# Cross attention and routed FFN on one core: another buffer order at the end of attention, two late loads of the first batch behind its context, and the second column chunk in reverse token order

## The reference

```python
def xattn(query, key):
    a = einsum('bqd,bkd->bqk', query, key)
    return einsum('bqk,bkd->bqd', softmax(a), key)

def ffn(x, base_w, base_b, A, B, router_w):      # base_w 2048x2048, A 64x2048, B 16x2048x64
    base_out = einsum('bsi,oi->bso', x, base_w) + base_b
    res_hidden = einsum('bsi,ri->bsr', x, A)
    probs = softmax(einsum('bsi,ei->bse', x, router_w))
    topw, topi = top_k(probs, 2); topw = topw / (sum(topw) + 1e-6)
    combine = sum(one_hot(topi, 16) * topw[..., None], axis=-2)
    return base_out + 0.5 * einsum('bse,bsr,eor->bso', combine, res_hidden, B)

x = x + xattn(layernorm(x), ctx)
x = x + ffn(layernorm(x), ...)
```

## Time and profile before

| | |
|---|---|
| time, median of 3 runs | 1458.26 us (1456.08 to 1459.49) |
| the profiled execution: its time, its span | 1453.22 us, 1451.5 us |
| PE busy | 1365.1 us, 94% of the span |
| DVE, ACT, POOL busy | 950.6, 634.3, 325.4 us |
| mean granted PE clock | 0.985 |
| mean DMA rate | 242 GB/s |

### The profile page before, as it was taken

How to read it: one execution, slowest core, us unless ns; L and a number is a source line. 1 busy time by engine, 2 the same in 40 slices (tenths; PEclk the granted TensorE clock), 3 DMA queues, 4 the chain that set the end, 5 groups by cost and what they waited for, 6 DMA issues and landing times.

```text
span 1451.5 us, 18409 instructions
## 1 busy us (share of the span) xinstructions
PE 1365.1 (94%) x6777; PEld 1107.6 (76%) x6777; DVE 950.6 (65%) x1199; ACT 634.3 (44%) x797; POOL 325.4 (22%) x247
## 2 busy tenths in 40 slices
PE   5899999999999999999799988899989999999998
PEld 4678787787878787787688766677767788888886
DVE  6486777777687767768355467676767746445553
ACT  3355554545564554545311266677767501100100
POOL 2002002020201102020414724444445011111110
PEclk9899999999999999999999999999999999999999
DMA  9958678687867768679656698999996987887874
GB/s 323 271 179 261 198 255 252 202 249 235 276 213 250 231 223 253 211 251 178 198 166 173 185 280 268 264 313 293 302 308 166 359 250 240 254 256 240 257 246 130
DMA packets 216840, 350.59 MB, mean 242 GB/s; under 512 B 26992, under 2 KB 129392, under 8 KB 207088
## 3 DMA queue, kind: packets, MB, share of 16 engines
q1 hardware_dynamic: 198192, 282.31, 64.5%
q0 software_dynamic: 10528, 52.85, 11.7%
q10 hardware_dynamic: 8064, 14.68, 2.9%
HBM read 266.11 MB, written 99.41 MB: 252 GB/s over the span
## 4 chain that ended last, share of the span: by engine, by line
PE 35%; DMA 13%; DVE 3%; issue 2%; ACT 1%; SPq 1%; POOL 0%; POOLq 0%; ACTq 0%; DVEq 0%
PE scores L829 11%; PE scores L830 10%; PE scores L831 10%; DMA res<-x_scratch 7%; DMA y_scratch<-y_out,yrow_i 3%; DMA w_in<-in_wT_dram 2%; PE work L865 1%; PE work L866 1%; DMA a_in<-xT_scratch 1%; DVE w_l L1382 1%; DVE raw_l L1148 1%; ACT y_out L1054 1%; ACT b_hl L1046 0%; DMA hs_scratch<-hg,pos_i 0%; DVE x L1184 0%
## 5 line engine op out<-in xcount | busy, mean ns | idle before, releaser
L829 PE MATMUL scores<-w_h,a_h 128*128 128x512 f32 x896 | 354.5, 396 | 14.0 <-DVE a_l L1389 8.1
L831 PE MATMUL scores<-w_h,a_l 128*128 128x512 f32 x896 | 352.4, 393 | 0.0
L830 PE MATMUL scores<-w_l,a_h 128*128 128x512 f32 x896 | 352.4, 393 | 0.0
L1030 ACT ACTIVATE a_h<-a_in 128x512 fp32r<-128x512 f32 x168 | 94.3, 621 | 317.5 <-DMA a_in<-xT_scratch 210.5
L1389 DVE TENSOR_TENSOR a_l<-a_in,a_h 128x512 fp32r<-128x512 f32 x168 | 130.7, 826 | 127.2 <-ACT a_h L1030 123.1
L829 PEld LDWEIGHTS scores<-w_h,a_h 128*128 128x128 f32 x896 | 169.7, 189 | 53.6 <-issue 15.2
L831 PEld LDWEIGHTS scores<-w_h,a_l 128*128 128x128 f32 x896 | 169.5, 189 | 38.3
L830 PEld LDWEIGHTS scores<-w_l,a_h 128*128 128x128 f32 x896 | 169.7, 189 | 37.1
L695 PE MATMUL scores<-ctxT_h,nT_h 128*112 128x494 f32 (+1 forms) x512 | 174.9, 342 | 10.6 <-DVE ctxT_l L1138 6.2
L1148 DVE TENSOR_TENSOR raw_l<-raw_in,val_h 128x512 fp32r<-128x512 f32 x192 | 155.0, 826 | 44.8 <-ACT val_h L959 44.6
L1557 POOL TENSOR_TENSOR res<-res,bias_b 128x512 f32<-128x512 f32 x56 | 86.4, 1543 | 407.9 <-DMA res<-x_scratch 388.0
(11 more groups left out here) (149 smaller groups left out, 1977.8 us busy)
## 6 DMA issues: line engine op xcount, KB each, us to landing
ctxT_in<-in_ctxT_dram SPq DMA_DIRECT2D x64, 750.0 KB, 7.6
a_in<-xT_scratch SPq DMA_DIRECT2D x42, 1024.0 KB, 8.7
raw_in<-in_ctx_dram SPq DMA_DIRECT2D x32, 1280.0 KB
w_in<-in_wT_dram SPq DMA_DIRECT2D x32, 512.0 KB, 9.6
x<-in_x_dram SPq DMA_DIRECT2D x8, 1792.0 KB, 9.3
xT_scratch<-xT_st SPq DMA_DIRECT2D x8, 1792.0 KB, 11.8
res<-x_scratch SPq DMA_DIRECT2D x56, 256.0 KB, 7.7
y_add<-y_scratch SPq DMA_DIRECT2D x56, 256.0 KB, 5.3
```

The lines of the kernel that those rows point to most:

```text
L829: pe.matmul(o, ah, wh, start=(k == 0), stop=False)
L830: pe.matmul(o, ah, wl, start=False, stop=False)
L831: last = pe.matmul(o, al, wh, start=False, stop=(k == KD - 1))
```

## The change

Four edits of the order, with the same arithmetic:

1. **Buffer order.** `w_h` moves from in front of `a0` to between `a1` and `a2`. `a0` then lies under nothing of the values, `a1`'s load only over raw chunk 0, and the weights' high parts over raw chunks 0 to 3. So `load_a(0)` goes up in SP's queue, to directly behind the last four weight loads of the first eight, ahead of the fill of `hs_scratch` and of the stores of `xT` and `hn`; `load_a(1)` takes the place that `load_a(0)` had, and `load_a(2)` is the first token load after attention. Token tile 0 is split in quarters behind steps 9 to 12, five weight pairs behind steps 15, 17, 19, 21 and 22, and the last three pairs in tile 0 of the FFN, on ACT ahead of token tile 1 and of the layer norm of the last batch. In tile 1 token tile 2 is split ahead of the copies of `x2T_last` (before: behind them). `y_add` and `late_y` move into the place of `a2`.
2. **Late values of the first batch.** `load_raw(0, 2)` and `load_raw(0, 3)` are issued behind context pairs 6 and 7, no longer behind 4 and 5.
3. **Reverse order.** Chunk 1 visits the token tiles from 13 down to 0. Its first three visits (14, 15, 16) find their tiles in place, and so do the first two visits of the paired part (28, 29): five of the 42 token loads go, with their 20 copies and 20 subtractions. `step_of(g)` takes over where `tile_of(g)` was used as a counter.
4. SP waits for `tile_done` only where it loads a token tile.

```diff
-FIRST_W_AT = (8, 10, 12, 14, 16, 18, 20, 22)
-FIRST_A_AT = 23
+FIRST_W_AT = (15, 17, 19, 21, 22)
+FIRST_A_AT = (9, 10, 11, 12)
...
     def tile_of(g):
+        if g >= PAIRED:
+            return (g - PAIRED) // 2
+        return g if g < TT else 2 * TT - 1 - g
...
-    A_SLOT = [v % AR if v < PAIRED else 1 + (v - PAIRED) % 2 for v in range(VISITS)]
-    A_USE = [A_SLOT[:v + 1].count(A_SLOT[v]) for v in range(VISITS)]
+    A_FIRST, A_SLOT = list(range(TT)), [v % AR for v in range(TT)]
+    for v in range(TT, VISITS):
+        back = AR if v < PAIRED else 2
+        turn = TT if v < PAIRED else PAIRED
+        if v - turn < back:
+            A_FIRST.append(A_FIRST[2 * turn - 1 - v])
+            A_SLOT.append(A_SLOT[2 * turn - 1 - v])
+        else:
+            A_FIRST.append(v)
+            A_SLOT.append(A_SLOT[v - back])
+    A_NEW = [v for v in range(VISITS) if A_FIRST[v] == v]
...
-        w_h = sb("w_h", [P, WR, WP, BANK], F32R)
         for i in range(AR):
+            if i == AR - 1:
+                w_h = sb("w_h", [P, WR, WP, BANK], F32R)
...
-                    if first and j - LR + 2 < CH:
-                        load_raw(0, j - LR + 2)
+                    if first and j - LR in (2, 3):
+                        load_raw(0, j - LR)
...
                     for j in range(PAIRS // 2, PAIRS):
                         load_w(j)
+                    sp.wait_ge(xT_stored, (NB - 2) * 16)
+                    load_a(0)
                     sp.wait_ge(fresh_ready, 2)
...
-                    sp.wait_ge(val_used, b * (CH * NT) + 2 * NT)
-                    sp.wait_ge(xT_stored, (NB - 2) * 16)
-                    load_a(0)
+                    sp.wait_ge(val_used, b * (CH * NT) + NT)
+                    load_a(1)
...
             sp.wait_ge(val_used, NB * CH * NT)
-            load_a(1)
...
                 if g < PAIRED:
-                    at_least(sp, tile_done, g)
-                    load_a(g + 2)
+                    if g + 2 in A_NEW:
+                        at_least(sp, tile_done, g)
+                        load_a(g + 2)
...
                 if g == 0:                          # ACT
+                    for j in range(len(FIRST_W_AT), PAIRS):
+                        if j == 6:
+                            act.wait_ge(val_used, NB * CH * NT)
+                        weight_high(j)
+                    tile_high(1, range(KD // AQ))
                     for n in range(CH):
                         normalise_last(n)
-                    act.wait_ge(val_used, NB * CH * NT)
-                    tile_high(1, range(KD // AQ))
                     continue
                 if g == 1:
+                    tile_high(2, range(KD // AQ))
                     for n in range(NX):
                         x2T_last(n)
...
                 if g == 0:                          # DVE
+                    weight_low(5)
                     last_stats()
+                    weight_low(6)
                     shift(mv2, rs2, nb2, rstd2, bias2, NB - 1)
+                    weight_low(7)
                     tile_low(1, range(KD // AQ))
                     continue
+                finish(g - 1)
                 if g == 1:
+                    tile_low(2, range(KD // AQ))
                     for n in range(NX):
                         x2T_last(n)
-                finish(g - 1)
```

More of the change, by code:

```diff
@@ L103, in tile_of, with step_of @@
     def tile_of(g):
+        if g >= PAIRED:
+            return (g - PAIRED) // 2
+        return g if g < TT else 2 * TT - 1 - g
+    def step_of(g):
         return g % TT if g < PAIRED else (g - PAIRED) // 2
@@ L107, in visit_of @@
         return g if g < PAIRED else PAIRED + (g - PAIRED) // 2
-    A_SLOT = [v % AR if v < PAIRED else 1 + (v - PAIRED) % 2 for v in range(VISITS)]
-    A_USE = [A_SLOT[:v + 1].count(A_SLOT[v]) for v in range(VISITS)]
+    A_FIRST, A_SLOT = list(range(TT)), [v % AR for v in range(TT)]
[9 more added lines that the diff above has]
+    A_NEW = [v for v in range(VISITS) if A_FIRST[v] == v]
+    A_LOAD = [A_NEW.index(A_FIRST[v]) for v in range(VISITS)]
+    A_USE = [len([u for u in A_NEW if u <= v and A_SLOT[u] == A_SLOT[v]]) for v in range(VISITS)]
+    Y_SLOT = AR - 1
+    assert all(A_SLOT[v] != Y_SLOT for v in range(PAIRED, VISITS))
     assert T % P == 0 and KD % AQ == 0 and 2 * T <= NOWHERE
@@ L285, in xattn_ffn_kernel @@
         assert y_over[0] <= SBUF_END
-        y_add = over(at_a0, "y_add", [P, 2, 2, BANK])
-        late_y = over(at_a0, "late_y", [P, 2, 2, BANK])
+        y_add = over(at_y, "y_add", [P, 2, 2, BANK])
+        late_y = over(at_y, "late_y", [P, 2, 2, BANK])
         def w_pair(n):
@@ L581, in load_late @@
             def load_late(n):
-                c, t = n // TT, n % TT
+                c, t = chunk_of(n), tile_of(n)
                 at_least(sp, late_stored[n % 2], n // 2 * 16)
@@ L627, in _ @@
             sp.wait_ge(val_used, NB * CH * NT)
-            load_a(1)
             sp.wait_ge(xT_stored, (NB - 1) * 16)
             for g in range(GT):
-                c, i = chunk_of(g), tile_of(g)
+                c, i = chunk_of(g), step_of(g)
                 if g < PAIRED:
-                    at_least(sp, tile_done, g)
-                    load_a(g + 2)
-                elif g >= PAIRED + 2 and c == EARLY and i + 1 < TT:
+                    if g + 2 in A_NEW:
+                        at_least(sp, tile_done, g)
+                        load_a(g + 2)
+                elif c == EARLY and visit_of(g) + 1 in A_NEW:
                     sp.wait_ge(tile_done, g)
@@ L996, in one @@
                         j = FIRST_W_AT.index(e)
-                        if j == 5:
-                            act.wait_ge(val_used, b * (CH * NT) + NT)
+                        if j == 0:
+                            act.wait_ge(val_used, b * (CH * NT) + 2 * NT)
+                        if j == 3:
+                            act.wait_ge(val_used, b * (CH * NT) + 3 * NT)
                         weight_high(j)
-                    if stage == "last" and e == FIRST_A_AT:
-                        act.wait_ge(val_used, b * (CH * NT) + 3 * NT)
-                        tile_high(0, range(KD // AQ))
+                    if stage == "last" and e in FIRST_A_AT:
+                        tile_high(0, (FIRST_A_AT.index(e),))
                     if stage != "last" and e in LN1_AT:
@@ L1026, in tile_high @@
             def tile_high(v, parts):
+                if v not in A_NEW:
+                    return
                 act.wait_ge(a_loaded[A_SLOT[v]], A_USE[v] * 16)
@@ L1097, in _ @@
                 if g < PAIRED:
-                    tile_high(g + 1, range(KD // AQ) if g in ROUTING else (0, 1))
+                    if g > 1:
+                        tile_high(g + 1, range(KD // AQ) if g in ROUTING else (0, 1))
                     store_tile(g - 1)
@@ L1119, in _ @@
                         expert_high(s + 2)
-                if g < PAIRED and g not in ROUTING:
+                if 1 < g < PAIRED and g not in ROUTING:
                     tile_high(g + 1, (2, 3))
@@ L1362, in one @@
                         weight_low(FIRST_W_AT.index(e))
-                    if not new and e == FIRST_A_AT:
-                        tile_low(0, range(KD // AQ))
+                    if not new and e in FIRST_A_AT:
+                        tile_low(0, (FIRST_A_AT.index(e),))
                     if new and e - 3 in QT_AT:
@@ L1384, in tile_low @@
             def tile_low(v, parts):
+                if v not in A_NEW:
+                    return
                 at = A_SLOT[v]
                 for q in parts:
-                    dve.wait_ge(a_high, v * (KD // AQ) + q + 1)
+                    dve.wait_ge(a_high, A_LOAD[v] * (KD // AQ) + q + 1)
                     cols = slice(q * AQ, (q + 1) * AQ)
@@ L1495, in _ @@
                     hidden_back("tail", NB)
-                if g < PAIRED:
+                if 1 < g < PAIRED:
                     tile_low(g + 1, range(KD // AQ) if g in ROUTING else (0, 1))
-                elif i + 1 < TT:
+                elif g >= PAIRED and i + 1 < TT:
                     tile_low(visit_of(g) + 1, (0, 1) if c == EARLY else (2, 3))
```

10 lines of the change are left out of this document (5 added, 5 removed).

## The result

| | before | after |
|---|---|---|
| time, median (runs) | 1458.86 us (6 runs, 1456.08 to 1461.41) | 1438.09 us (6 runs, 1436.78 to 1441.4) |
| ratio, 95% interval | | 0.9863 (0.9846 to 0.988) |
| profiled execution: time, span | 1453.22, 1451.5 us | 1436.82, 1433.4 us |
| mean granted PE clock | 0.985 | 0.989 |

The kernel became 20.8 us faster; the forecast was 20.5 us and 1437.8 us. The sum was right, but of its three terms only one was near its size, so that the total came this close is luck. In what follows a ratio is turned into microseconds with 1458.86 us.

A forecast was written before the change was run, and what follows sets the result against it. PE bounds quiet stretches, so only its waits could pay. 4.9 + 8.5 + 7.1 = 20.5 us, taken from the median of the runs, gave 1437.8 us; range 1429.5 to 1449 us.

The forecast's parts named there:

- Edit 2, 4.9 us: First batch: context pairs 6 and 7 land in time, saving 3.67 us of PE wait and 1.25 us of slow clock; bounds 2 and 5.5.
- The whole 3.67 us go: Scores of the first batch: PE's 3.67 us wait for context pair 6 disappears entirely.
- first batch gains nothing: First batch: the time goes into the softmax and first values, whose loads come late; 15.6 us gained, 1442.7; chance 0.08.
- Edit 1, 8.5 us: End of attention, FFN tiles 0 to 2: waits of 6.52 and 1.54 plus 2.5 of clock go, minus 2.0; bounds 6 and 10.5.
- The new wait for a transposed group: FFN tile 1, block 8: PE waits 2.0 us for the third transposed group, released by DVE's `nT_l`.
- the load work within the values: Last batch's values: earlier token tile 0 quarters and later weight pairs cost nothing, hidden under PE's 1.4 us per step.
- token tile 0 comes a little late: Last batch's values, behind step 9: a load five microseconds beyond the slack leaves 15.5 us gained, 1442.8; chance 0.07.
- the slower rival: Same place: token tile 0 served only with the `hs_scratch` fill and stores, stopping value copies and PE; up to 1463.8; chance 0.03.
- Edits 3 and 4, 7.1 us: Turn from chunk 0 to chunk 1 into tile 15: 2.4 + 2.7 + 2.0 us saved; bounds 2.4 and 11.6.
- the turn itself: Start of chunk 1: without two token quarters ahead, DVE makes the first weight pair ready 2.4 us earlier.
- The terms for tiles 14 and 15: Tile 14: 2.7 us from an earlier last weight pair; tile 15: 2.0 us, half of 4.0 us of waits on late scatters.
- the expert stage takes it back: Tiles 14 to 26: if bytes set the pace, waits only move to later scatters; 13.4 us stay, 1444.9; chance 0.18.

The follow-up runs named there:

- b_late_values: Kernel before with only raw chunks 2 and 3 of the first batch moved behind context pairs 6 and 7: 1460.31 us, ratio 1.0008 to the kernel before.
- b_reverse: Kernel before with only chunk 1 in reverse token order and 37 token loads, `y_add` in the third token buffer's place: 1445.69 us, ratio 0.9894 to the kernel before.
- a_early_values: Changed kernel with raw chunks 2 and 3 of the first batch back behind context pairs 4 and 5: 1439.77 us, ratio 0.9858 to the kernel before.
- a_transposes_first: Changed kernel with the copies of `x2T_last` ahead of token tile 2 again, on ACT and DVE: 1439.41 us, ratio 0.9859 to the kernel before.
- a_forward: Changed kernel with chunk 1 in forward order and all 42 token loads: 1452.15 us, ratio 0.9952 to the kernel before.
- before_again: The kernel before, unchanged, run once more for a second trace: 1463.68 us, span 1461.0 us.
- after_again: The changed kernel, unchanged, run once more for a second trace: 1432.34 us, span 1430.6 us.
- a_raw2_early: Changed kernel with the first batch's raw chunk 2 issued behind context pair 5 and chunk 3 behind the residual input: 1437.01 us, ratio 0.9845 to the kernel before.
- a_no_token_loads: Changed kernel without the 11 token loads of visits 17 to 27, copies and subtractions kept: 1406.49 us, ratio 0.9632 to the kernel before.
- a_idle_loads: Changed kernel plus three unused 1 MB transfers to DRAM in steps 12 to 14, where token loads were: 1445.97 us, ratio 0.9897 to the kernel before.
- a_best: Changed kernel with first-batch raw chunk 2 behind context pair 5, chunk 3 behind the residual load, `load_a(0)` before the last four weight loads: 1433.87 us, ratio 0.9812 to before.

## Why the prediction came true, point by point

**Edit 2, 4.9 us: wrong.** The step that failed is "The whole 3.67 us go". The pairs were in time, as predicted, and the values began some 4 us earlier (59.6 us, 59.7 in b_late_values, before 63.8), but the time did not stay gained. Two things were shown in its place. First, moving the two raw chunks back left DMA half idle from 30 to 35 us (0.46 of the time, against 1.07 before), and the 3 MB were issued at 34.84 and 38.95 us instead (before 23.85 and 28.75), in a queue that was full from there on (share 0.91 to 1.06 from 35 to 75 us), ahead of the residual input, whose landing took 24.8 us and not 16.5. PE's wait moved from 49 to 78 us: 2.47 us, and 3.28 in b_late_values. I had looked only at who first uses the raw chunks, and not at what else is queued behind them. Second, the 3.67 us is no fixed cost: it is in both traces of the kernel before (3.67 and 3.72), but only 0.69 us are left of it in b_reverse, and none in a_early_values, with the same order of loads there; why is not shown. One reading was off besides: the cost of a chunk was taken from the stretch from 50 to 55 us, where 259 GB/s are moved, but from 30 to 45 us, where pair 6 was loaded, it was 312 to 367. The rival "first batch gains nothing", which had 0.08, is what happened, with the late load at the residual input.

**Edit 1, 8.5 us: right, within its bounds.** From tile 0 to 2 the four traces with the old order take 34.8 to 36.0 us, mean 35.3, and the four with the new order 26.0 to 26.7, mean 26.4: 8.9 us. The new wait for a transposed group was there with the predicted releaser, 0.79 us and not 2.0. What I costed at nothing, the load work within the values, costs 1.4 us (42.0 to 43.4), because token tile 0 landed at 654 us and ACT asked for it 1.95 us earlier: the rival "token tile 0 comes a little late". It is mild in most traces (0.9 to 2.0 us), but in a_early_values and a_transposes_first, where ACT stood 4.12 and 4.52 us for that tile, the stretch is 3.6 and 4.5 us longer than before. Net 7.5 us by these traces and 7.0 by the ratio of a_forward. Its place in front of `hs_scratch` and the stores held up; the slower rival did not appear.

**Edits 3 and 4, 7.1 us: right in mechanism, half its size.** The ratios give 13.0 and 15.5 us. Of the terms: the turn itself was well sized, tile 13 with the wait behind it is 18.2 us in place of 20.5 in the trace that I read, 2.3 against 2.4 predicted (20.2 and 20.4 in before_again and b_late_values, but 19.4 in a_forward). The terms for tiles 14 and 15, together 4.7 us, were mis-sized. The time from tile 14 to 16 was 43.4 us in the trace that I read; in before_again, b_late_values and a_forward it is 45.2, 49.1 and 48.7; with the reverse order it is 37.6, 38.7, 38.6 and 38.8 (after, after_again, a_early_values, b_reverse), mean 38.4. Between the means that is 8.2 us. The spread is wide on this side too: a_transposes_first and a_raw2_early have 35.5 and 35.1.

Nor is the wait for the first expert result in tile 14 gone with the reverse order, as I had it: it is 0.56 us in the trace after, but 3.34 in after_again and 2.70 in b_reverse, against 2.74, 7.83, 8.68 and 3.23 with the forward order. What sets its end is ACT's copy of the last weight pair, as predicted. Counted from the start of tile 14 that copy begins at 10.6, 15.5, 18.9 and 18.5 us in the four forward traces, and at 9.9, 9.9, 10.4 and 10.9 in the four reverse ones: the trace that I read was the one in which the pair came early.

And the turn to the paired part, costed at nothing, gives 316.5 - 314.9 = 1.6 us, and no trace has less than 1.5. 2.3 + 8.2 + 1.6 = 12.1, near the 13.0.

The cause of the size is shown in part. Transfers set the pace from tile 16 to 26 (a_no_token_loads, 3.1 us for each load of 1 MB), and three transfers that nobody uses seem to take some 5 us back (a_idle_loads, not clear of the scatter). That was the premise of the rival "the expert stage takes it back", whose conclusion was wrong: where bytes set the pace, fewer bytes are a gain, and the time is not given back. From tile 16 to 28 the four traces with forward order take 221.6 to 228.7 us, mean 226.0, and the four with reverse order 224.9 to 226.4, mean 225.4. Against the one trace that I had, it looks as if 3.3 us were given back; that is the scatter of this stage. What of the rest belongs to ACT's and DVE's work was not tested.

**The sum.** That it came out is luck, the errors cancelled: 4.9 too much, 1.5 too much, and 6 to 8 too little. Between the two profiled executions the span fell by 18.1 us, in the columns of the table: 2.9 - 1.4 + 10.0 + 0.3 + 8.0 - 3.3 + 1.6. The 2.9 us up to `hidden` are not credited to edit 2, since a_early_values has them without it (634.9); what they are due to stays open, as does why the ratio of a_best is better than its trace. Of the signs that I had named, the bias adds that wait over 10 us from tile 13 to 26 fell by two, from 7 to 5, where I had said one; the wait of about 2.9 us at the turn came as 3.01; and two signs against the forecast showed: waits for `raw_l` at steps 10 and 12, 0.60 and 0.24 us, and waits of PE in tiles 16 to 26 that sum to 18.7 us, against 15.9 before. The second means little, since the other three traces with the forward order have 19.3 to 23.5 us.

## What to carry to other kernels

When a load is moved back to make way, list everything queued behind its new place and ask what DMA does in the hole that it leaves: a hole in a full queue can be paid for later by the last load in line. Where transfers set the pace, a load that a reversed loop order makes needless can be worth more than the stall that one trace shows at its place (here up to about 3 us for 1 MB in rows of 512 bytes; less where the transfers were put back alone, and 0.8 us each at the turn to the paired part). Read a wait that ends on a transfer from two or three traces before taking it as a term of a sum: tile 14 varied from 22.4 to 32.6 us with the same order.

## What the runs showed of the hardware

**How long an issue on SP lasts goes with what was issued in front of it.** The same 256 KB residual load stood in the queue for 0.43 us (after), 9.72 (a_idle_loads), 14.98 and 21.55 us (a_forward), always behind a transfer of 1 MB in the long cases, and put first it passed the wait on to the next issue, 23.70 us. The Trainium skill, "Perfetto Trace Analysis", section "What "DMA-bound" means", reads the slices on the issuing sequencer's track as descriptor generation, not data movement. The rows don't bear that out as the whole of it: one and the same instruction has 0.43 or 21.55 us, and the length goes with what was issued ahead.

**The same stall costs PE's clock differently.** Behind the wait at the turn, 3.00 or 3.01 us in each of these traces (after, shown above with a granted clock of 0.51, then b_reverse, a_no_token_loads, a_best and after_again, each over the first 6 us of tile 14):

```profile
863.60:869.60 6.00, 6.00 (x19) 4.78 (x20) 5.85 (x6) 2.12 (x3) 0.69 (x1) 0.72 1.03 337
```
```profile
855.80:861.80 6.00, 5.99 (x19) 4.80 (x20) 5.85 (x6) 3.07 (x4) 0.70 (x1) 0.72 1.06 355
```
```profile
853.10:859.10 6.00, 5.96 (x20) 4.81 (x21) 5.85 (x6) 2.16 (x4) 0.73 (x1) 0.74 1.03 364
```

```profile
852.25:858.25 6.00, 6.00 (x26) 4.96 (x27) 5.85 (x6) 3.19 (x4) 0.69 (x1) 1.00 1.04 363
```

In the first four PE falls to the lower level of 1.2 GHz: 6 us at 0.51 lose 2.9 us, and 6 us at 0.72 to 0.74 lose 1.6 to 1.7. In the last it keeps 2.4 GHz throughout. How much of this reaches the time is another matter: after_again, which lost nothing to the clock here, waited 3.34 us for the first expert result later in tile 14, where the trace after has 0.56, and its tile 14 took 22.2 us against 21.1. A faster PE only came earlier to a place where it had to wait.
